# A cross-attention and expert-FFN kernel on one core: small matmuls put beside the first scores, statistics taken earlier, identity transposes in the first step

## What is computed

```python
# x [32,256,256], ctx [32,77,256], mask [32,77]
kv_rows = concat(layernorm(ctx), layernorm(layernorm(x)))   # 77 + 256 keys
q = rmsnorm(latents @ W_q); k, v = split(kv_rows @ W_kv); k = rmsnorm(k)
attn = softmax(where(mask, -big, q @ k.T)) @ v              # 4 heads of 64
x = x + attn @ W_out + b_out
h = layernorm(x)
scores = sigmoid(h @ gate.T)        # 8 experts, 2 groups, the best group's top 2
cw = 2.5 * chosen / sum(chosen)
routed = sum_e cw[:, e] * relu(h @ up_e.T)**2 @ down_e.T    # every expert is computed
x = x + routed + relu(h @ shared_up.T)**2 @ shared_down.T   # shared FFN of 512
```

## Time and profile before

| | us |
|---|---|
| median of 3 runs | 1163.17 (1162.99 to 1163.61) |
| the profiled execution, its own time | 1166.36 |
| span of its trace | 1164.6 |
| TensorE (PE) busy | 1149.4 |
| VectorE (DVE) busy | 1005.6 |
| ScalarE (ACT) busy | 800.1 |
| GpSimd (POOL) busy | 542.9 |

### The profile page before, as it was taken

How to read it: one execution, slowest core, us unless ns; L and a number is a source line. 1 busy time by engine, 2 the same in 40 slices (tenths; PEclk the granted TensorE clock), 3 DMA queues, 4 the chain that set the end, 5 groups by cost and what they waited for, 6 DMA issues and landing times. The chain is left out here.

```text
span 1164.6 us, 32989 instructions
## 1 busy us (share of the span) xinstructions
PE 1149.4 (99%) x11772; PEld 1074.1 (92%) x11772; DVE 1005.6 (86%) x3511; ACT 800.1 (69%) x1896; POOL 542.9 (47%) x466
## 2 busy tenths in 40 slices
PE   7999999999999999999999999999999999999997
PEld 7799999999999999999999999999999999999997
DVE  6788888889988889988888988889888899888887
ACT  6567776676866667766677766678766678666673
POOL 3344545444545444445445444445454445454432
PEclk9899999999999999999999999999999999999999
DMA  5000000000000000000000000000000000000000
GB/s 186 2 14 23 23 23 11 23 14 24 22 23 10 23 14 22 24 22 11 14 23 23 23 19 16 13 22 23 22 12 22 14 23 22 23 10 24 2 10 19
DMA packets 28145, 26.06 MB, mean 22 GB/s; under 512 B 6544, under 2 KB 27440, under 8 KB 27984
## 3 DMA queue, kind: packets, MB, share of 16 engines
q1 hardware_dynamic: 27904, 23.83, 6.6%
q0 software_dynamic: 80, 0.14, 0.0%
HBM read 15.57 MB, written 8.39 MB: 21 GB/s over the span
## 5 line engine op out<-in xcount | busy, mean ns | idle before, releaser
L1311 POOL TENSOR_TENSOR hid_lo<-relu,hid_hi 128x512 fp32r<-128x512 f32 x191 | 246.7, 1292 | 251.8 <-DVE hid_hi L1069 167.2
L295 PE MATMUL down_ps<-down_hi,hid_hi 128*128 128x256 f32 x768 | 234.2, 305 | 2.8 <-DVE acc L1091 2.6
L1091 DVE SCALAR_TENSOR_TENSOR acc<-down_ps,route_w,acc 128x256 f32<-128x256 f32 x512 | 221.8, 475 | 6.9 <-PE down_ps L297 6.2
L295 PE MATMUL up_ps<-x_hi,up_hi 128*128 128x256 f32 x768 | 227.5, 296 | 0.0
L297 PE MATMUL down_ps<-down_hi,hid_lo 128*128 128x256 f32 x768 | 216.6, 282 | 0.0
L296 PE MATMUL down_ps<-down_lo,hid_hi 128*128 128x256 f32 x768 | 216.1, 281 | 0.0
L296 PE MATMUL up_ps<-x_lo,up_hi 128*128 128x256 f32 x768 | 214.9, 280 | 0.0
L297 PE MATMUL up_ps<-x_hi,up_lo 128*128 128x256 f32 x768 | 214.7, 280 | 0.0
L676 ACT ACTIVATE probs<-masked,neg_max,q_scale 128x333 f32<-128x333 f32 x256 | 168.1, 658 | 1.1 <-DVE neg_max L930 1.1
L723 ACT ACTIVATE relu_sb<-up_ps 128x512 f32<-128x512 f32 x192 | 113.6, 592 | 72.8 <-PE up_ps L297 69.5
L295 PEld LDWEIGHTS down_ps<-down_hi,hid_hi 128*128 128x128 f32 x768 | 144.9, 189 | 15.6 <-issue 15.1
(11 more groups left out here) (148 smaller groups left out, 2838.7 us busy)
## 6 DMA issues: line engine op xcount, KB each, us to landing
out<-acc SPq DMA_DIRECT2D x31, 256.0 KB, 2.2
x_first<-in_x SPq DMA_DIRECT2D x16, 256.0 KB, 2.8
w_stage<-in_x SPq DMA_DIRECT2D x16, 256.0 KB, 2.8
up_stage<-in_up_t SPq DMA_DIRECT2D x1, 1536.0 KB, 6.4
down_stage<-in_down_t SPq DMA_DIRECT2D x1, 1536.0 KB, 7.9
c_first<-in_ctx SPq DMA_DIRECT2D x16, 77.0 KB
w_stage<-in_ctx SPq DMA_DIRECT2D x16, 77.0 KB
w_stage<-in_w_kv SPq DMA_DIRECT2D x1, 512.0 KB, 5.0
```

The lines of the kernel that those rows point to most:

```text
L295: nc.tensor.matmul(out_ap, s_hi, m_hi, start=first, stop=False)
L1091: nc.vector.scalar_tensor_tensor(acc[:, t, :], down_ps[:, (e + 1) % 2, t * D:(t + 1) * D], route_w[:, t, e:e + 1], acc[:, t, :], ALU.mult, ...
L1311: nc.gpsimd.tensor_tensor(hid_lo[:, p % HID_RING, :], relu2[:, p % 2, :], hid_hi[:, p % HID_RING, :], ALU.subtract).then_inc(hid_lo_done, 1)
```

## The change

On TensorE the sums of squares and the router come after `up` 0 and 1, right ahead of score pair 0, and write into `down_ps` (banks 0 and 1) in place of `attn_ps`. Their waits change with that: they wait for the last additions of the FFN before (`acc_done`), score pairs 0 and 1 no longer wait for `q_norm_done` and `exp_neg_done`, and the shared down and `down` 0 do instead. `transpose_x2` moves ahead of `down` 6. `up` 0 waits for the first half of x2_lo at its start and for the second half at its fourth matmul. In the tail the router comes after `up` 0 and 1 as well.

In step 0 twelve identity transposes come between `transpose_k` and the sums, two ahead of each of `transpose_probs` 4 to 7, four ahead of `project_out`; six come ahead of `transpose_k` of step 1.

On ACT the squares of q come after the four x2 copies, and `router_exp` after the first hidden block. On DVE x2_low is taken in halves around the second part of `k_normalize`; `q_norms` comes after `k_low` of the next step; the statistics of a batch are taken a whole step earlier, in three pieces around `attn_out` (step 1, which has no predecessor with that place, takes those of batch 2 after the first negated maximum). On POOL the second `hidden_low` waits for the first negated maximum.

```diff
@@ -345,2 +345,4 @@
         pe.wait_ge(head_sel_done, 1)
+    elif b > 1:
+        pe.wait_ge(acc_done, (b - 1) * ACC)
     for t in range(T):
@@ -348,3 +350,3 @@
             for tile in COLUMN_TILES:
-                last = nc.tensor.matmul(attn_ps[tile, 0, t * H + 2 * ft:t * H + 2 * ft + 2],
+                last = nc.tensor.matmul(down_ps[tile, 0, t * H + 2 * ft:t * H + 2 * ft + 2],
                                         q_sq[:, ft, t * P + tile.start:t * P + tile.stop], head_sel[:],
@@ -371,9 +373,5 @@
     if pair == 0:
-        pe.wait_ge(q_norm_done, b + 1)
         pe.wait_ge(k_hi_done, (b + 1) * FT)
         pe.wait_ge(k_lo_done, (b + 1) * FT)
-    elif pair == 1:
-        if experts:
-            pe.wait_ge(exp_neg_done, b)
-    else:
+    elif pair > 1:
         pe.wait_ge(masked_done, b * U + u - 2)
@@ -390,2 +388,4 @@
 def transpose_probs(b, u):
+    if b == 0 and u >= 4:
+        keep_warm(2)
     pe.wait_ge(prob_done, b * U + u + 1)
@@ -459,2 +459,4 @@
         pe.wait_ge(gate_in, DMA)
+    else:
+        pe.wait_ge(acc_done, b * ACC)
     pe.wait_ge(x2_full_done, (b + 1) * FT)
@@ -464,3 +466,3 @@
             for tile in COLUMN_TILES:
-                last = nc.tensor.matmul(attn_ps[tile, 3, t * E:(t + 1) * E],
+                last = nc.tensor.matmul(down_ps[tile, 1, t * E:(t + 1) * E],
                                         x2_full[:, k, t * P + tile.start:t * P + tile.stop],
@@ -475,3 +477,3 @@
         pe.wait_ge(x2_hi_done, (b + 1) * FT)
-        pe.wait_ge(x2_lo_done, (b + 1) * FT)
+        pe.wait_ge(x2_lo_done, b * FT + 1)
     if p == 1 and following:
@@ -483,2 +485,4 @@
             cols = slice((2 * p + j) * P, (2 * p + j + 1) * P)
+            if p == 0 and j == 0 and k == 1:
+                pe.wait_ge(x2_lo_done, (b + 1) * FT)
             last = split_product(up_ps[:, (p + 1) % 2, j * S:(j + 1) * S], (up_hi[:, k, cols], up_lo[:, k, cols]),
@@ -500,2 +504,4 @@
             pe.wait_ge(acc_done, b * ACC)
+        if b + 1 < B:
+            pe.wait_ge(q_norm_done, b + 2)
     for f in range(FS):
@@ -512,4 +518,4 @@
         pe.wait_ge(acc_done, b * ACC + 2 * e - 1)
-    elif not first:
-        pe.wait_ge(acc_done, b * ACC - 2)
+    else:
+        pe.wait_ge(exp_neg_done, b + 1)
     for t in range(T):
@@ -532,3 +538,9 @@
+    if b == 1:
+        keep_warm(6)
     transpose_k(b)
+    if first:
+        keep_warm(12)
+    ffn("up", 0)
+    ffn("up", 1)
     sum_q_squares(b, first)
@@ -536,4 +548,2 @@
         router(f, f_first)
-    ffn("up", 0)
-    ffn("up", 1)
     score_pair(b, 0, experts)
@@ -584,2 +594,4 @@
     project_kv(b + 1, 1)
+    if first:
+        keep_warm(4)
     project_out(b, 0, following)
@@ -589,4 +601,4 @@
     project_q(b + 1)
-    ffn("down", 6)
     transpose_x2(b)
+    ffn("down", 6)
     ffn("down", 7)
@@ -606,5 +618,5 @@
 steps(step)
-router(B - 1, False)
 up(B - 1, 0, False, False)
 up(B - 1, 1, False, False)
+router(B - 1, False)
 up(B - 1, 2, False)
@@ -645,2 +657,5 @@
     nc.scalar.activation(q_hi[:], qv, ACT.Copy).then_inc(q_hi_done, 1)
+
+def q_square(b):
+    qv = up_ps[:, 0, :].rearrange("p (f s) -> p f s", f=FT)
     nc.scalar.activation(q_sq[:], qv, ACT.Square).then_inc(q_sq_done, 1)
...
@@ -737,5 +752,5 @@
     k_high(b, first)
+    ffn(0)
     if experts:
         router_exp(f, f_first)
-    ffn(0)
     if first:
@@ -776,2 +791,4 @@
     x2_high(b, first)
+    if following:
+        q_square(b + 1)
...
@@ -813,2 +831,6 @@
 def stats_first(b):
+    stats_rows(b)
+    stats_context(b)
+
+def stats_rows(b):
     dve.wait_ge(x_loaded[b % 2], (b // 2 + 1) * DMA)
...
@@ -988,4 +1012,4 @@
-def x2_low(b):
-    for ft in range(FT):
+def x2_low(b, *parts):
+    for ft in parts or range(FT):
         dve.wait_ge(x2_full_done, b * FT + ft + 1)
@@ -1127,2 +1151,3 @@
     k_low(b, 1)
+    q_norms(b, first)
     if first:
@@ -1130,4 +1155,2 @@
         up_parts(0)
-    if following and not first:
-        layer_norm1(b + 1, False)
     mask_scores(b, 0, first)
@@ -1137,2 +1160,4 @@
     negate_max(b, 0)
+    if b == 1:
+        layer_norm1(b + 1, False)
     if following and not first:
@@ -1196,3 +1221,7 @@
     add(4)
+    if not first and b + 2 < B:
+        stats_rows(b + 2)
     attn_out(b, first)
+    if not first and b + 2 < B:
+        stats_context(b + 2)
     attn_low(b, 0)
@@ -1202,2 +1231,4 @@
         down_parts(2)
+    if not first and b + 2 < B:
+        aggregate_first(b + 2, False)
     residual_half(b, 0)
@@ -1211,7 +1242,7 @@
     k_normalize(b + 1, 0, False)
+    x2_low(b, 0)
     k_normalize(b + 1, 1, False)
-    x2_low(b)
+    x2_low(b, 1)
     q_low(b + 1)
     add(6)
-    q_norms(b + 1, False)
     add(7)
@@ -1242,3 +1273,2 @@
 q_low(0)
-q_norms(0, True)
 dve.wait_ge(gamma_done, 1)
@@ -1321,5 +1351,7 @@
     q_scales(b, first)
+    low(0)
     if first:
         rstd_first(1, False)
-    low(0)
+    if experts:
+        pool.wait_ge(neg_max_done, b * T + 1)
     low(1)
```

More of the change, by code:

```diff
@@ L589, in step @@
                 project_q(b + 1)
+                transpose_x2(b)
                 ffn("down", 6)
-                transpose_x2(b)
                 ffn("down", 7)
@@ L716, in router_exp @@
                     act.wait_ge(router_step, (b - 1) * ROUTER_STEPS + 1)
-                nc.scalar.activation(exp_neg[:], attn_ps[:, 3, 0:T * E].rearrange("p (t e) -> p t e", t=T),
+                nc.scalar.activation(exp_neg[:], down_ps[:, 1, 0:T * E].rearrange("p (t e) -> p t e", t=T),
                                      ACT.Exp, scale=-1.0).then_inc(exp_neg_done, 1)
@@ L792, in _ @@
             q_out(0, True)
+            q_square(0)
             for cols in UP_COLS[1:]:
@@ L795, in _ @@
             steps(step)
+            hidden(B - 1, 0, False)
             router_exp(B - 1, False)
-            hidden(B - 1, 0, False)
             for p in range(1, PAIRS):
@@ L816, in stats_first, with stats_context @@
                     nc.vector.bn_stats(stats1[:, t, :], x_in[b % 2][:, t, :]).then_inc(ln1_step, 1)
+            def stats_context(b):
                 dve.wait_ge(c_loaded[b % 2], (b // 2 + 1) * DMA)
@@ L880, in q_norms @@
                     dve.wait_ge(q_scale_done, b)
-                nc.vector.tensor_scalar(q_norm[:], attn_ps[:, 0, 0:U], DH * RMS_EPS * RMS_EPS, None,
+                nc.vector.tensor_scalar(q_norm[:], down_ps[:, 0, 0:U], DH * RMS_EPS * RMS_EPS, None,
                                         ALU.max).then_inc(q_norm_done, 1)
```

## The result

| us | before | after |
|---|---|---|
| median | 1163.33 (1162.99 to 1163.61, 4 runs) | 1171.82 (1171.11 to 1172.37, 4 runs) |
| ratio, 95% interval | | 1.0066 (1.0054 to 1.0078) |
| the profiled execution, its span | 1166.36, 1164.6 | 1171.11, 1169.2 |

A forecast was written before the change was run, and what follows sets the result against it. TensorE, busy 1149.4 of 1164.6 us, was taken as the bound, with DVE close behind. Terms -5.9 + 0.5 - 1.5 + 0.6 = -6.3 us took the median 1163.17 to 1156.9 us, range 1155.4 to 1158.4, chance 0.60.

The forecast's parts named there:

- q_norm, q_scale, and the wait of the second hidden_low: Delayed by 1.5 us in each step, covered by up 2 and 3 and two score visits; no cost counted.
- the x2 copies come no sooner: Rival: late x2 copies delay k_rms part 2 and transpose_k, 0.26 us lost a step, 1170.9 us; chance 0.06.
- Joined visit, 0.19 us a step: Sums and router joined ahead of scores, steps 1 to 31: stalls 0.30 for 0.49, 5.9 us gained; transpose_k every 35.10.
- the seam: Router to scores, between two part-array tile shapes: 0.11 to empty plus 0.09 for first score weights, 0.20 us.
- the free and the dear seam: Router to scores: wholly free, 1150.7, left outside the rivals; or full way out and in, 0.30, 1160.0, chance 0.05.
- DVE must come along: In each step k_lo must end by 617.58; it was expected at 617.30, a margin of 0.28 us.
- The rival on k_lo: Scores still wait for k_lo at the old time, nothing gained per step, 1162.8 us; chance 0.07.
- That on k_rms: Rival of late x2 copies delaying k_rms part 2, chance 0.06; PE waiting for k_rms in steady steps was a wrong-sign.
- Statistics: Statistics leaving DVE between k_lo and the masks for later waits: nothing on PE, but masks come sooner.
- keep_warm(4), +0.5: Four identity transposes before project_out in step 0 lie on the way: 0.5 us added.
- The clock in step 1, -1.5: Granted clock expected to stay up in step 1 with added work: 1.5 us gained, bounds 0 and 1.7.
- The tail, +0.6 within 0 to 1.3: Later router beside POOL's first hid_lo: its third operation held, delaying DVE's hid_lo and the shared down, 0.6 us added.

The follow-up runs named there:

- number 11: Changed kernel with GpSimd's residual x_res made to wait for group_sel, the router's 12th step: 1166.0 us, ratio 1.001.
- numbers 2: Changed kernel without POOL's wait of the second hidden_low for the first negated maximum: 1208.11 us, ratio 1.0368.
- number 10: Changed kernel with a wait added on GpSimd, the second hidden_low starting only after sig_den, the router's first step: 1204.18 us, ratio 1.0333.
- number 14: Number 13 with the tail order of the change instead of the old one: 1160.97 us, ratio 0.9971.
- number 12: Changed kernel with both waits, the second hidden_low behind sig_den and x_res behind group_sel: 1173.45 us, ratio 1.0076.
- number 9: Changed kernel with the next batch's statistics back in front of the masks in every step: 1220.67 us, ratio 1.048.
- number 4: Changed kernel with POOL's third hidden_low also waiting for the router's 12th step, the group choice: 1167.44 us, ratio 1.0025.
- numbers 13: Changed kernel with third hidden_low behind routing, x_res ahead of rstd_first, batch 2's statistics before neg_max, old tail order, only keep_warm(6) kept: 1161.38 us, ratio 0.998.
- 15: Number 14 with the tail's router ahead of the up slices and writing attn_ps, as in the kernel before: 1160.84 us, ratio 0.9964.
- number 8: Kernel before with only the statistics moved two batches ahead, those of batch 2 staying in front of step 1's masks: 1164.22 us, ratio 1.0001.
- number 7: Changed kernel with batch 2's statistics in step 1 moved in front of q_norms and the first neg_max: 1171.58 us, ratio 1.006.
- number 5: Changed kernel without any of its added identity transposes (four keep_warm calls out): 1170.72 us, ratio 1.0061.
- before again: Kernel before, run and profiled once more with no edit: 1164.86 us, span 1163.1 us.
- number 3: Changed kernel with sums of squares back behind transpose_k in attn_ps, q_norm behind add(6), no POOL wait for neg_max: 1172.1 us, ratio 1.0056.

## Why the prediction was wrong

**The step that failed** is the term put at nothing for "q_norm, q_scale, and the wait of the second hidden_low": they "are delayed by 1.5 us; their cover is up 2 and 3 and two score visits". The prediction asked of GpSimd's passes only who waits for their output on TensorE, and there the cover held: in steps 3 and 4 of the changed kernel no TensorE wait is put down to GpSimd. It did not ask what VectorE does while they run, though it priced just that, one operation for 1.15 us, in the tail. The sums now come 3.6 us into the step, q_scale takes GpSimd until 5.96, and the first two hidden_low move from 4.98 and 6.65 to 5.92 and 7.31, on top of the routing that had had a gap to itself. q_scale's 1.64 us is a GpSimd operation that the text named and never priced. The routing is held there for 0.70 and 1.10 us in a normal step, and a third time in a long one. That this is the cause, and not only what the trace shows beside it, the waits tell: number 11 takes away one meeting and the long steps fall by 1.0 to 1.1 us, numbers 2 and 10 add meetings and nearly all steps grow to 36.6, and in number 14, where the routing meets one pass and mask 4 comes at 9.85, the steps reach 35.11.

What the routing's delay costs can be read off over all kernels; mask 4 in us of the step:

| kernel, step | mask 4 | behind 10.87 | step |
|---|---|---|---|
| number 14, normal | 9.85 | none | 35.11 |
| after, normal | 10.95 | 0.08 | 35.19 |
| number 12 | 11.23 | 0.36 | 35.47 |
| number 11, step 3 | 11.33 | 0.46 | 35.59 |
| number 10 | 12.35 | 1.48 | 36.6 |
| after, steps 3, 11, 19, 27 | 12.40 | 1.53 | 36.65 |
| number 9 | 12.90 | 2.03 | 37.15 |

In these rows a step with the joined visit takes 35.11 us plus what mask 4 is behind 10.87. The kernel before had 0.16 us more room: its steps stay at 35.27 with mask 4 at 10.99 and take 35.45 with 11.19 (step 13). So against the shortened step VectorE was a second bound with nothing in hand, which the text said only of k_lo. Two cases don't fit, the normal steps of number 4 (9.86, 35.25) and steps 3, 11, 19 and 27 of numbers 13 to 15 (10.35, 35.31). There the delay falls behind mask 4, and the adds show it: in number 14 they end at 21.36 us of step 3 and the slice starts at 21.51, against 20.89 and 21.30, without a wait, in step 4.

The measured 1171.8 us lies near the 1170.9 of the rival "the x2 copies come no sooner". That is chance: the rival has every step lose 0.26 us at transpose_k, and no normal step waits there.

**Point by point.**
- *Joined visit, 0.19 us a step.* The mechanism was right, the seam too: the router takes 0.37 us to the scores (159.20 to 159.57) where the sums take 0.27, and the first score matmuls 0.26 where the next take 0.15. That is 0.21 for the seam, with 0.20 taken, and rules out the free and the dear seam. 0.165 measured, and 35.11 where VectorE is in time (forecast 35.10). In the changed kernel 0.08 is left in normal steps, four steps lose 1.38 each against before, and steps 5, 21 and 29 lose 0.07 to 0.15.
- *DVE must come along.* Right: k_lo ends at 3.82 us, 0.39 ahead of the scores, and transpose_k flows into up without a wait. The rival on k_lo did not take place. That on k_rms did in a small way: in steps 5, 13, 21 and 29 its second part starts 0.15 us late and the fifth transpose 0.17 us late with it (0.55 us into the step for 0.39), which the prediction had named as a sign of being wrong.
- *Statistics.* "Nothing on PE" by themselves (number 8), as the prediction said, and without them the joined visit loses far more (number 9). In step 1, where they moved behind neg_max, they cost 1.6 us (number 7).
- *keep_warm(4), +0.5.* Measured 0.47. The others cost nothing that can be seen: step 0 is 27.31 without any of them, 27.32 to 27.40 with keep_warm(6) alone.
- *The clock in step 1, -1.5.* The clock stayed up, but the reason is not borne out (number 5), and the step showed no gain because the statistics took as much. The size is right for an execution with the fall (37.17 against 35.68), but before again has none, and the term was taken off a median of which nobody knew how many executions had it.
- *The tail, +0.6 within 0 to 1.3.* Measured +0.77 to +1.07, all three traces with the clock's fall. By numbers 14 and 15, both without it, the new order costs 0.87. PE, DVE and POOL in the tail of the changed kernel:

```profile
1148.24 0.44 PE L467 MATMUL down_ps<-gate_stage,x_full 128*32 128x8 f32 x32
...
1152.90 0.36 PE L295 MATMUL down_ps<-down_hi,hid_hi 128*128 128x256 f32 x1 [1.20 <-issue]
```

```profile
1148.97 1.21 DVE L1037 TENSOR_SCALAR sig_den<-exp_neg 128x16 f32<-128x16 f32 x1 [2.58 <-ACT exp_neg L732]
...
1152.11 0.69 DVE L1099 TENSOR_TENSOR hid_lo<-relu,hid_hi 128x512 fp32r<-128x512 f32 x1
```

```profile
1148.86 1.30 POOL L1341 TENSOR_TENSOR hid_lo<-relu,hid_hi 128x512 fp32r<-128x512 f32 x1 [7.91 <-ACT relu L746]
```

  The chain is the forecast one, but for the operation held: the first of the routing, for 1.21, and not the third. DVE's hid_lo waits its turn behind the routing, and the shared down starts 0.10 us behind its end, after 1.20 us of idle TensorE. The cost lies between the 0.6 taken and the upper bound.

The Trainium skill, "SBUF — State Buffer", Who interferes with whom, states the lock as going to the first to issue, for its whole instruction. By that rule 0.02 us decides over 1.1 us, and the traces agree: sig_den at 162.65 passes ahead of the hidden_low of 162.67, at 126.10 it does not pass that of 126.03. (Nearer than that the recorded starts don't tell: number 4's operation at 165.71 was held by a pass recorded at 165.72.)

**What stays open.** Why the second var comes 0.07 to 0.20 us late in steps 3, 11, 19 and 27. It does so in every kernel that has both parts of the change, and in none that lacks one (before, numbers 3, 8 and 9). The trace of the changed kernel has a transfer of instructions 8.0 to 8.3 us into these four steps, right behind the slip; but the kernels without the slip have it there too, at 8.1 to 8.7 us, and that it is the cause was not tried. Open as well is why the second part of k_rms comes 0.15 us late in steps 5, 13, 21 and 29, in every kernel with the change's order but number 9; there a transfer of instructions follows at 0.6 to 0.9 us of the step.

## What to carry to other kernels

When a change moves work on GpSimd, even a wait or a tiny operation in front of the big ones, list what VectorE runs beside every big pass before and after, and count up to one full pass for each small operation of the kinds below that falls in. Where the routing of a batch has to fit between passes, fix the order with a wait behind the whole small sequence (numbers 4, 11, 14), not behind its first operation (number 10), and then look at what the delayed pass meets instead (number 4): a race won by 0.02 us was lost in 4 of 29 steps here. Look for the second chain's slack at its own next meeting with TensorE, and compare with more than one trace of the kernel before, with the granted clock of the stretch beside each length.

## What the runs showed of the hardware that was not expected

- Which small VectorE operations are held beside a GpSimd pass of 128x512: sig_den, a tensor with a constant (0.15 to 1.26), neg_max (0.16 to 0.83 in number 3), comparisons of 128x2 (0.16 to 1.28), and one of 128x128 (0.29 to 1.43, number 4). The masks, which read PSUM, run beside them at 0.50 us as ever, and the reciprocal at 0.25.
- GpSimd's power on 128x3 (rstd, 0.85 us) holds nobody in the normal step: from 165.59 to 166.44 VectorE's small operations go on at 0.15 to 0.17, and mask 4 starts.
- The same power on 128x8 (q_scale) takes 1.64 us, more than a subtraction of 128x512 (1.30).
- The part ahead of the first transpose_k takes 18.4 to 20.0 us from one profile to the next, and not by kernel: 18.57 in the changed kernel, 20.03 in number 7, which has the same instructions up to there. Against differences of one or two us a single profile's total says little; its normal steps, which mostly repeat within 0.05 us, say more.
- The granted clock falls to 0.50 for a stretch of the tail in some traces and not in others (number 5 against the changed kernel, the same tail: 57.25 and 58.26 us). The page's row of 40 slices shows a 9 there all the same.
